# Three exact bf16 terms for the relation table and its sums, in a graph and attention kernel

## The reference, cut to what matters

```
def _L1_gnn_ref(x, edge_index, edge_type, weight, bias):
    row, col = (edge_index[0], edge_index[1])
    xt = jnp.einsum('ni,rio->rno', x, weight)
    messages = xt[edge_type, col]
    out = jax.ops.segment_sum(messages, row, num_segments=num_nodes)
    return jax.nn.relu(out + bias)
...
xn = _layernorm(x, axis=-1)
x = x + _L1_gnn_ref(xn, ...) + _L1_mix_ref(xn[None], ...)[0]
```

## Time and profile before

| | us |
|---|---|
| runs of before, median of 3 (lowest, highest) | 7969.41 (7962.21, 7973.39) |
| span of the profiled execution | 7942.4 |
| TensorE busy in it | 5581.7 (70%) |
| VectorE busy | 5151.1 (65%) |
| GpSimd busy | 3471.0 (44%) |
| ScalarE busy | 1874.7 (24%) |

### The profile page before, as it was taken

How to read it: one execution, slowest core, us unless ns; L and a number is a source line. 1 busy time by engine, 2 the same in 40 slices (tenths; PEclk the granted TensorE clock), 3 DMA queues, 4 the chain that set the end, 5 groups by cost and what they waited for, 6 DMA issues and landing times. The chain is left out here.

```text
span 7942.4 us, 87092 instructions
## 1 busy us (share of the span) xinstructions
PE 5581.7 (70%) x25066; PEld 3810.3 (48%) x25066; DVE 5151.1 (65%) x11656; ACT 1874.7 (24%) x4564; POOL 3471.0 (44%) x3440
## 2 busy tenths in 40 slices
PE   5877773555555655528799788887999999960991
PEld 2446652333333433314454334443777777750661
DVE  6467777888888877764367566666666666660332
ACT  0333332222223332212134200000222222220220
POOL 0000005777777777700000455555666667625006
PEclk8998886677777777759899899998998999965995
DMA  4100004444555555510013322222333333332223
GB/s 145 42 26 1 1 1 105 124 123 124 125 127 130 134 130 129 126 38 0 17 78 132 112 68 70 71 72 72 89 95 87 89 95 95 92 77 80 63 64 107
DMA packets 310174, 665.89 MB, mean 84 GB/s; under 512 B 77964, under 2 KB 173950, under 8 KB 302701
## 3 DMA queue, kind: packets, MB, share of 16 engines
q0 software_dynamic: 180352, 455.22, 22.7%
q1 hardware_dynamic: 129367, 205.30, 7.5%
HBM read 546.51 MB, written 113.55 MB: 83 GB/s over the span
## 5 line engine op out<-in xcount | busy, mean ns | idle before, releaser
L2026 POOL DMA_INDIRECT ag_rows<-table,row_src x1612 | 1594.9, 989 | 2007.2 <-POOLq L2813 1052.5
L1123 POOL DMA_INDIRECT at_rows<-table,row_dst x1612 | 1633.9, 1014 | 491.0 <-issue 448.9
L1289 PE MATMUL at_p_a<-at_rows,at_hot 128*125 128x264 f32 x3224 | 1137.0, 511 | 997.3 <-issue 976.8
L1289 PEld LDWEIGHTS at_p_a<-at_rows,at_hot 128*125 128x125 f32 x3224 | 708.6, 246 | 1184.9 <-issue 1045.2
L1252 DVE TENSOR_TENSOR acc<-acc,at_p_a 125x264 f32 x1612 | 687.4, 426 | 244.3 <-PE at_p_a L1289 101.4
L2388 PE MATMUL mo_p_e<-ag_rows,ag_hot 128*125 128x256 f32 x2192 | 651.0, 422 | 265.0 <-DVE acc L2232 231.5
L2232 DVE TENSOR_TENSOR acc<-acc,mo_p_e 125x256 f32 x1096 | 459.3, 419 | 498.7 <-PE mo_p_e L2388 308.0
L2388 PEld LDWEIGHTS mo_p_e<-ag_rows,ag_hot 128*125 128x125 f32 x2192 | 392.0, 199 | 480.3 <-DVE acc L2232 376.3
L2136 DVE TENSOR_TENSOR mo_prod<-mo_far,mo_twice 125x256 f32<-125x256 f32 x1600 | 580.1, 419 | 50.9 <-issue 44.3
L1075 POOL PARTITION_ALL_REDUCE sb_top<-sb_top x1 | 0.4, 397 | 1220.5 <-DVE sb_top L1046 1220.5
L1239 DVE TENSOR_TENSOR at_rows<-at_rows 128x1024 f32<-128x1024 f32 x496 | 496.9, 1022 | 21.8 <-ACT at_rows L1171 21.5
(11 more groups left out here) (475 smaller groups left out, 9944.2 us busy)
## 6 DMA issues: line engine op xcount, KB each, us to landing
at_wide<-node_t SPq DMA_DIRECT2D x124, 406.2 KB
table<-rt_row SPq DMA_DIRECT2D x50, 1000.0 KB
at_rows<-table,row_dst POOLq DMA_INDIRECT x1612
ag_rows<-table,row_src POOLq DMA_INDIRECT x1612, 2.8
moe_in<-ones SPq DMA_DIRECT2D x1, 13440.0 KB
ex_space<-moe_in SPq DMA_DIRECT2D x105, 128.0 KB, 2.2
moe_out<-ex_space SPq DMA_DIRECT2D x105, 128.0 KB, 1.7
table<-row SPq DMA_DIRECT2D x50, 128.9 KB
```

Of the source, the lines that this page charges most:

```text
L1123: pool.indirect_dma_start(out=rows[n % 3][:, g, :], out_offset=None, in_=m.table0, in_offset=bass.IndirectOffsetOnAxis(ap=row_i[:, n * G + ...
L1289: pe.matmul(p_a[k % BANKS][0:P, 0:TW], hot[n % 2][:, g, :], rows[n % 3][:, g, :], start=True, stop=True).then_inc(s_agg, 1)
L2026: pool.indirect_dma_start(out=rows[:, i % RING, j, :], out_offset=None, in_=m.table1, in_offset=bass.IndirectOffsetOnAxis(ap=row_i[:, 2 * ...
```

## The change

The table in DRAM holds for each value three bf16 numbers in place of one f32: high, middle and low, whose sum is the value. A row grows from 1024 to 1536 bytes.

In `relation_table` the high part is ScalarE's copy of the bank to bf16. TensorE then subtracts it in the bank, by a product of the high part with a negative identity matrix `minus` in bf16 that accumulates. ScalarE copies what is left to bf16, the middle part, and VectorE subtracts this from the bank, which gives the low part. The stage now goes pair by pair: step j has the products of pair j and the rest of the work of pair j-1. `table_plan` has a step for each pair, and VectorE takes part in it. In `relational_mix` the one-hot is bf16 with 128 columns in place of 125, each f32 product becomes three bf16 products that accumulate, and the ring has 9 pairs.

```
-        row = [sb(f"rt_row{u}", [P, R, C], F32) for u in range(2)]
+        row = [sb(f"rt_row{u}", [P, R, 3, C], BF16) for u in range(2)]
+        minus = sb("rt_minus", [P, P], BF16)
...
                 for n in range(NT):
-                    sp.wait_ge(s_bank, 4 * n + 4)
-                    sp.dma_start(m.table1.rearrange("(n r) c -> n r c", r=R)[n * P:n * P + P, :, :],
-                                 row[n % 2][:, :, :]).then_inc(s_out[n % 2], 16)
+                    sp.wait_ge(s_low, 4 * n + 4)
+                    sp.dma_start(m.table1.rearrange("(n r) c -> n (r c)", r=R)[n * P:n * P + P, :],
+                                 row[n % 2][:, :, :, :].rearrange("p r k c -> p (r k c)")).then_inc(s_out[n % 2], 16)
...
+                    for j in range(last + 1):
+                        n = j // 4
+                        if j < last:
+                            if j % 4 == 0:
+                                if n + 1 < NT:
+                                    copy_xt(n + 1)
+                                if n >= 2:
+                                    act.wait_ge(s_out[n % 2], 16 * (n // 2))
+                            act.wait_ge(s_mm, j + 1)
+                            act.copy(term(j, 0), pair(j)).then_inc(s_high, 1)
+                            if j % 4 == 1 and n + 2 < NT:
+                                norm(n + 2)
+                        if j >= 1:
+                            act.wait_ge(s_left, j)
+                            act.copy(term(j - 1, 1), pair(j - 1)).then_inc(s_mid, 1)
                         yield
...
+                def row_work():
+                    for j in range(last + 1):
+                        if j >= 1:
+                            dve.wait_ge(s_mid, j)
+                            dve.tensor_tensor(term(j - 1, 2), pair(j - 1), term(j - 1, 1), ALU.subtract).then_inc(s_low, 1)
+                        yield
...
+                        if j >= 1:
+                            pe.wait_ge(s_high, j)
+                            pe.matmul(p_w[(j - 1) % 4][0:P, :], minus[:, :], term(j - 1, 0), start=False, stop=True, skip_group_check=True
+                                      ).then_inc(s_left, 1)
...
-RING = 13
+RING = 9
...
-        rows = sb("ag_rows", [128, RING, 2, C], F32)
-        hot = [sb(f"ag_hot{u}", [128, HOTS, P], F32) for u in range(2)]
+        rows = sb("ag_rows", [128, RING, 2, 3 * C], BF16)
+        hot = [sb(f"ag_hot{u}", [128, HOTS, 128], BF16) for u in range(2)]
...
-                            mm = pe.matmul(p_edge[bank[i]][0:P, C * j:C * j + C], hot[i // 2 % 2][:, 2 * (i % 2) + j, :],
-                                           rows[:, i % RING, j, :], start=True, stop=True)
+                            for k in range(3):
+                                mm = pe.matmul(p_edge[bank[i]][:, C * j:C * j + C], hot[i // 2 % 2][:, 2 * (i % 2) + j, :],
+                                               rows[:, i % RING, j, C * k:C * k + C], start=k == 0, stop=k == 2)
-        m.table1 = nc.dram_tensor("table1", (R * N, C), F32).ap()
+        m.table1 = nc.dram_tensor("table1", (R * N, 3 * C), BF16).ap()
```

More of the change, by code:

```diff
@@ L1723, in table_plan @@
     plan, done, sort_steps = [], 0, SORTED - sum(LOCAL)
-    for n in range(NT):
+    for j in range(4 * NT):
         plan.append("rows")
-        while done < sort_steps * (n + 1) // (NT - 2) and done < sort_steps:
+        while done < sort_steps * (j + 1) // (4 * (NT - 2)) and done < sort_steps:
             plan.append("sort")
             done += 1
-    return plan + ["sort"] * (sort_steps - done)
+    return plan + ["rows"] + ["sort"] * (sort_steps - done)
 def relation_table(nc, m, w, row_i, node_f):
@@ L1745, in relation_table @@
         p_k = [ps(f"rt_p_k{k}", [128, 512]) for k in range(2)]
-        s_xn, s_tr, s_xt, s_mm, s_bank = (sem("rt_" + x) for x in (
-            "s_xn", "s_tr", "s_xt", "s_mm", "s_bank"))
+        s_xn, s_tr, s_xt, s_mm, s_high, s_left, s_mid, s_low, s_minus = (sem("rt_" + x) for x in (
+            "s_xn", "s_tr", "s_xt", "s_mm", "s_high", "s_left", "s_mid", "s_low", "s_minus"))
         s_out = [sem(f"rt_s_out{u}") for u in range(2)]
@@ L1750, in relation_table @@
         plan = table_plan()
+        last = 4 * NT
+        term = lambda j, k: row[j // 4 % 2][:, 2 * (j % 4):2 * (j % 4) + 2, k, :]
+        pair = lambda j: p_w[j % 4][0:P, :].rearrange("p (r c) -> p r c", r=2)
         with m.block() as block:
@@ L1870, in sort_work @@
                     yield
-                weave([x for x in plan if x == "sort"], sort=sort_work())
+                weave(plan, sort=sort_work(), rows=row_work())
             @block.tensor
@@ L1885, in row_work @@
                     pe.wait_ge(m.s_table_w, 32)
+                    pe.wait_ge(s_minus, 1)
                     turn(0)
[L1887 to L1893, removed]
+                    for j in range(last + 1):
+                        n, k = j // 4, j % 4
+                        if j < last:
+                            if k == 0:
+                                if n + 1 < NT:
+                                    turn(n + 1)
+                                pe.wait_ge(s_xt, n + 1)
+                            if j >= 4:
+                                pe.wait_ge(s_low, j - 3)
                             for c in range(2):
```

11 lines of the change are left out of this document (6 added, 5 removed).

## The result

The changed kernel takes **8345.42 us** (median of 4 runs, 8336.0 to 8356.79) against 7971.4 of the kernel before beside it (4 runs): a ratio of **1.0472**, 95% interval 1.0458 to 1.0487. The forecast was 8226 in a range of 8100 to 8370. The profiled spans are 7942.4 and 8334.3 us, so 392 us are to be found. The medians are 374 us apart, so some 18 of the 392 lie in which execution was profiled.

The account below looks back on a forecast made before the run. Table writes and TensorE were taken to bound the table stage, TensorE to be nearest the bound in the sums. Median 7969.4 + 402 (table) - 145 (sums) = 8226 us, range 8100 to 8370.

Parts of the forecast that it names:

- One write in flight: Table stage: a tile's write is never issued before the write of the tile before it has landed.
- The first rival: Table stage: writes queue up after all, only five engines count, +192 us, end at 8016 us; chance 10%.
- The size of the period: Table stage: table writes 16.0 us apart as a serial chain, so the stage loses 402 us.
- The landing: Table stage: a 1.536 MB write takes 13.9 us from issue to landing, 1.05 of it after the bytes.
- The steps behind it: Table stage, after a landing: two ScalarE copies 1.07 us, VectorE's subtraction 0.70, SyncE's issue and semaphores 0.3.
- the tail: End of the table stage: from the issue of tile 48 at 4828 to the last bytes at 4854.
- Products in bf16: Relational sums: three bf16 instructions of 106 ns replace an f32 product, saving 109 ns a chunk if weight loads stay hidden.
- I take three quarters: 145 us gained: Relational sums, both parts: of 194 us of TensorE time saved, 145 arrive, with ends of 97 and 194.
- the third rival: Compute no longer fits under the table write, or the sums give little: 8293, or 8366 with half the gain; 13%.
- The faster rival: Table stage: larger rows spread over more engines, stage only +45 to +80 us, end near 7890; chance 8%.
- The fit that the prediction took there: Table write: about 2.0 us plus bytes over 436 GB/s, a landing of 5.5 us, which would make the faster rival true.
- Writes and TensorE are both the bound: Table stage before: five engines take 7.7 us a tile of 7.82, TensorE busy 381 of 388 us; added bytes can't hide.

Follow-up runs that it names:

- 1: Changed kernel with ScalarE's middle copy of a tile's last pair moved ahead of the wait for the write before the last: 8255.13 us, ratio 1.0363.
- 2: Changed kernel with each tile's table write split into two transfers of 112 and 13 partitions: 8106.85 us, ratio 1.0193.
- 3: Kernel before with a ring of 9 pairs in place of 13, nothing else: 7967.57 us, ratio 0.9994.
- 4: Changed kernel with the third bf16 product of each chunk done twice, so four products: 8271.22 us, ratio 1.0386.
- 10: The kernel of 9 with a fourth bf16 product per chunk, by a tile of zeros: 7936.97 us, ratio 0.9980.
- 9: Changed kernel with writes of 112 and 13 partitions, middle copy ahead of the wait, and VectorE's load of tile numbers moved later: 7957.19 us, ratio 0.9988.
- 7: Changed kernel without the low part, rows of 1 KB, third product repeating the middle part: 8681.92 us, ratio 1.0189, on another chip.
- 11: Kernel before with writes of 112 and 13 partitions and VectorE's load of tile numbers moved later: 7862.38 us, ratio 0.9875.
- 8: Changed kernel with the bf16 one-hot 125 columns wide, products into 125 rows: 8867.92 us, ratio 1.0420, on another chip.
- 5 to 8: Four runs, of edits to the changed kernel and one to the kernel before, on another chip where the kernel before takes 8514.96 us.

## Why the prediction was right, and where it was not

**One write in flight: right.** All 48 waits are there, the share fell to 0.25 (forecast 0.22), and the edits of 1 and 2 each shorten the period. The first rival (writes in a queue) is refuted by the share and the count of waits; even with the order mended, writes are 12.6 us apart and not 11.6.

**The size of the period: 15.0 for 16.0.** From the first issue to the 49th it is (4782.17 - 4062.87)/48 = 14.99 us. The landing took 13.04 for the 13.9 of the sum: I took 1.05 us from the last bytes to the release where the windows show about 0.5, and the bytes were through 12.6 us after the issue and not 12.85. The steps behind it took 1.82 for 2.1. With the tail of 24.8 us for 26 the stage lost 355 us for 402. This term was 47 us too large.

**Products in bf16: right in their price.** 109 or 110 ns each at full clock for the forecast 106, loads hidden, the subtraction 0.69 for 0.70. A gather of 1.5 KB took a median of 946 ns, as before, and the ring costs nothing (3). Part one gained 50 of a forecast 54.

**Part two: the step that failed.** "I take three quarters: 145 us gained": 91 of these lay in part two, which lost 88 instead. I took TensorE's clock in the sums as given, and its saving as something to be collected. The rows in hand had 0.94 there, and a fall to 0.50 in a pause of the table stage; the prediction used that for the third rival, in the table alone, and gave it no price in the sums. The runs show in its place: 425 us more at 1.2 GHz. That it is the clock, and that more work of TensorE brings it back, is shown by 4 against the changed kernel and by 10 against 9: only products are added, and the low time falls from 591 or 696 us to 156, and from 466 to 121. That it isn't the larger gather is shown by 4 and 7, the ring by 3.

**The two errors had opposite signs:** the table 47 us better than forecast, the sums 183 worse (a loss of 38, where 145 were to be gained). Together 136 of the span: 8334.3 was measured, 7942.4 + 402 - 145 = 8199.4 forecast, a difference of 135. The median lies 11 us above the profiled span, where the forecast had carried over 27, and 135 - 16 = 119 us is the miss of the time. That the range held the time is in part luck: its upper end was drawn for the third rival, in which half of the sums' gain is left and TensorE's clock sets the period of the table. The period was the write's, and in the sums nothing was left of the gain; had the table cost the forecast 402 us, the time would have been 8392, outside the range.

**The faster rival** needed more engines for the write. The change as it stands doesn't give them, and 2 and 9 show what the stage would be with them: the sums begin 80 and 66 us later than before, where the rival had +45 to +80. The fit that the prediction took there from the Trainium skill, "DMA: Bandwidth & Descriptors", section "Anatomy of one DMA — SWDGE (gpsimd) path", is given for transfers that GpSimd issues, and these are SyncE's. The estimate of 5.5 us by it is near the 6.6 us of the write in pieces (2) and far from the 13.0 with five engines.

**"Writes and TensorE are both the bound"** is too strong: in 11 the last write lands in 4.3 us in place of 11.2, and the period doesn't move. The writes were some 0.1 us a tile away from binding (7.7 of 7.82 by the prediction's numbers), which is why 512 KB more made them bind.

**What stays open:** why a low stretch can last some 30 us while TensorE is busy throughout, why three bf16 products a chunk leave it low for longer than f32 products or four, and why the changed kernel has 32 long pauses in part two where the kernel before has 22. No run varied the pauses alone on one chip with the changed kernel beside it.

## What to carry to other kernels

A wait for an outgoing transfer belongs behind the last step that completes the transfer before it; otherwise a double buffer holds one transfer. Count what a transfer's shape makes of its engines before its bytes: 112 + 13 partitions in place of 125 took a write from 13.0 us to 6.6. And read the granted clock stage by stage before a saving on that engine goes into a sum: the time saved can come back as time at half speed, and a run with useless work added, as 4 and 10 here, tells it apart from the bytes and the data.

## What the runs showed of the hardware that was not expected

- TensorE at 1.2 GHz for 29.6 us with 29.34 us busy, after a pause of 2.08 us; stretches up to 38 us. The Trainium skill, "TensorE: Matmul & The Clock Gate", section "HAM oscillation — how this bites in real kernels", tells of waits after which the work starts at the low level. The rows agree with that start (0.50 behind the pause of 2.08 us).
- A third more products made a kernel 74 us faster (4), with real data as operand, and with zeros part two became 85 us shorter (10).
- A bf16 weight load of 125 columns took a median of 137 ns (8), one of 128 columns 98 ns (the changed kernel).
- Chips differ: the kernel before takes 7957 to 7971 us beside most runs here, and 8515 on the chip of 5 to 8.
- A write of 125 partitions kept five of sixteen DMA engines busy (0.31, 134 GB/s); as 112 and 13 partitions it reached 0.95 and 344 GB/s.
